# Value and ones products of the causal attention cores: five blocks a group become two

## The chip, the cores and the metric

One NeuronCore of a Trainium2 chip runs the whole kernel in one launch. The metric is the device time of a run in microseconds; what is compared is the median over several runs. Five engines work side by side, each through its own queue in order, and wait for each other by semaphores: TensorE (matrix products into eight PSUM banks), VectorE, ScalarE, GpSimd, and SyncE, which only issues DMAs. A product reads a stationary operand of up to 128 rows and 128 columns, and its output has as many partitions as the stationary operand has columns.

## The reference, cut to what matters

A decoder block on x of shape (4, 512, 512), float32:

```
x = x + causal_attention(layernorm(x), 16 heads of 32)            # "first"
x = x + cross_attention(layernorm(x), ctx, 32 heads of 16)        # "cross"
h = x + causal_attention(rms(x) * w, rotary q and k, 16 heads)    # "rotary", biases on q, k, v
x = h + experts(rms(h)) + shared_expert(rms(h))                   # top 2 of 8, and one shared
```

A causal attention is, per batch and head,

```
scores = q @ k.T / sqrt(32), masked where key > query
out    = softmax(scores) @ v
```

and a projection by a 512 x 512 matrix follows over all heads.

## The kernel before, in words

For each attention there is a projection phase (q, k, v, stored to memory as high and low parts) and a core phase, `core_phase` (line 915). The change lies in the core phase of the two causal ones, "first" and "rotary"; the code is shared with "cross".

A causal core works through 16 groups (`GROUPS`): 4 batches times 4 sets of 4 heads. A group has 16 steps, one for each pair of key tile m (0 to 3, 128 keys each) and head j (0 to 3), `step = 4 * m + j`. All engines run the same loop over groups and steps, and the order on TensorE is written out at lines 1286 to 1304. At each step it issues:

- `scores` (line 1152, products at L1162) of a tile 26 steps ahead: queries by keys, only for the maximum of each row. VectorE reduces it in `tile_max` (L1398; a second record, the accumulator read, ends it). Three PSUM banks hold these scores, so a score waits for the maximum of the tile three before it. Tiles are 128, 256, 384 and 512 columns wide.
- `scoresT` (line 1180, products at L1200, then the mask as a product with the identity at L1203): the transposed scores of this group with the row maxima subtracted through extra rows of the stacks. The keys' tile m has 512 - 128 m queries left; for m = 2 two heads and for m = 3 all four share one bank and one step (steps 8, 10, 12). ScalarE takes the exponential (L1350) into `prob_of[m]`. Three further banks rotate over these, the transposed maxima and the output projections (`share_banks`).
- at step 8, `max_transpose` (L1176) of the next group's maxima. GpSimd splits them first (`split_max`, L1597 and L1599), ScalarE copies them out (L1319) and broadcasts them by a DMA at step 9 into the next group's stack (`send_max`, L1097), which the next group's first `scoresT` waits for.
- blocks of **value products** (`values`, line 1231, L1241): four heads, each 32 output columns, so that together they fill the 128 partitions of bank 5; key tile m covers 512 - 128 m query columns, accumulated over m. Every float32 product shows as two records, so a block is 8 records.
- blocks of **ones products** (`ones_product`, line 1206, L1209): the same form with ones in place of v, the softmax's sums, into bank 6. `sums_of_first` takes key tile 0's first 128 queries; `sums` takes the other 384 columns from `total`, in which GpSimd adds the probabilities of all key tiles (`add_keys`, L1579). In the last group `sums_at_end` takes the sums straight from the probabilities, tile by tile.
- `project` (L1258): the output projection of the batch before, in thirds of four products, at steps 6, 7, 10 and 12, 14, 15 of the second and third group of a batch (the first batch has none before it).

VectorE follows a group's sums: at step 5 it flips the sums out of bank 6 (`flip_sums`, L1413), at step 6 it inverts and transposes them (`normalise`, L1420, L1423), at step 7 it scales bank 5 into `attn` (`scale`, L1433). The first value product of a group waits for that scaling of the group before, and the first ones product for the flip.

Which block stands where is set by `VALUES_LAG = 9` and `SUMS_STEP = 4` (line 987) through `values_behind` (line 1006): key tile 0 behind step 9 (with `sums_of_first`), tile 1 behind step 13, tile 2 behind step 1 of the next group, tile 3 behind step 5, and `sums` behind step 4. A step's scores and transposed scores are issued before its block.

```
VALUES_LAG, SUMS_STEP = 7 if cross else 9, 4
n, beat = divmod(g * N16 + step - VALUES_LAG, HEADS_AT_ONCE)
return divmod(n, TT) if beat == 0 and 0 <= n < GROUPS * TT else None
```

SyncE loads the stacks (`next_stack`, L213) three groups ahead, once the last transposed score of the group whose slot they take has run (step 12), and stores the projected rows (`store`, L1115); the order on its queue is fixed. ScalarE loads values (L1082), residual rows (L1090) and output weights.

Of the kernel before, what the change touches and what calls it, by code (L numbers as in the profile page):

```python
# [26 lines left out]
TT = S // P  # L27
# [887 lines left out]
def core_phase(nc, s, c, psum, a):  # L915
# [6 lines left out]
    cross, causal, dh, G = t.cross, t.causal, t.dh, t.groups  # L922
    BODY = a.body
    GROUPS = G * BODY
    N16 = TT * HEADS_AT_ONCE
    ctx = ExitStack()
    with ctx:
# [56 lines left out]
        PACKED = {2: 2, 3: 4} if causal else {}  # L984
        heads_in = lambda step: PACKED.get(step // HEADS_AT_ONCE, 1)
        leads = lambda step: step % heads_in(step) == 0
        VALUES_LAG, SUMS_STEP = 7 if cross else 9, 4
        bank_score, bank_shared = ((0, 1, 2, 3), (4, 5, 7)) if cross else ((0, 1, 2), (3, 4, 7))
        bank_o, bank_sum = (6, 6) if cross else (5, 6)
        N_SCORE = len(bank_score)  # L990
# [9 lines left out]
        def scores_before(step):  # L1000

            if cross:
                return range(step - 2, step + 2) if step % HEADS_AT_ONCE == 2 else ()
            return (step,)

        def values_behind(g, step):

            n, beat = divmod(g * N16 + step - VALUES_LAG, HEADS_AT_ONCE)
            return divmod(n, TT) if beat == 0 and 0 <= n < GROUPS * TT else None

        def probability(g, m, j):

# [4 lines left out]
        def tile_ahead(g, step):  # L1017

            n = g * N16 + step + AHEAD
            return divmod(n, N16) if n < GROUPS * N16 else None  # L1020
# [41 lines left out]
        with nc.Fori(0, B // BODY) as loop:  # L1062
            rows = lambda m, bi: m[bass.ds((loop * BODY + bi) * S, S), :].rearrange("(t p) d -> p t d", p=P)
            with nc.Block() as block:
# [86 lines left out]
                def _(pe):  # L1151
                    def scores(g, i):

                        m, j = divmod(i, HEADS_AT_ONCE)
                        n, slot = g * N16 + i, g % STACK_SLOTS
                        at, r = j // HALVES, j % HALVES * HALF_ROWS
                        bank = psum[bank_score[n % N_SCORE]]
                        if i == 0:
                            pe.wait_ge(stack_loaded[slot], 16 * (a.stacks_before + t.loads_of_stack * (g // STACK_SLOTS + 1)))
                        if n >= N_SCORE + EARLY:  # L1160
                            pe.wait_ge(s.max_done, maxima_made(n - N_SCORE) + 1)
                        last = nc.tensor.matmul(bank[:, 0 : width_q(m)], q_stack[slot][r : r + PRODUCT_ROWS, at, m * P : (m + 1) * P],  # L1162
                                                k_stack[slot][r : r + PRODUCT_ROWS, at, 0 : width_q(m)], start=True, stop=True)
                        last.then_inc(s.scores_ready, 1)
# [7 lines left out]
                    def max_transpose(g):  # L1172
                        pe.wait_ge(s.max_split, 2 * g)
                        free_bank(("max", g))
                        for m in range(TT):
                            last = nc.tensor.transpose(psum[bank_at["max", g]][0 : 2 * HEADS_AT_ONCE, m * P : (m + 1) * P],  # L1176
                                                       max_parts[:, m, :].bitcast(F32), c.ident[:])
                        last.then_inc(s.max_transposed, 1)

                    def scoresT(g, i):  # L1180

                        if not leads(i):
                            return
                        m, j0 = divmod(i, HEADS_AT_ONCE)
                        n, slot, heads = g * N16 + i, g % STACK_SLOTS, heads_in(i)
                        bank, q0 = psum[bank_at["score", n]], start_k(m)
                        tiles = bank[:, 0 : heads * (S - q0)].rearrange("p (h n) -> p h n", h=heads)
                        if i == 0:
                            if g == 0:
                                pe.wait_ge(a.carried.picks_here, 16 * (a.picks_before + HALVES * t.slots_at_hand))  # L1190
                            if g == t.slots_at_hand:
                                pe.wait_ge(s.picks_loaded, 16 * HALVES * (STACK_SLOTS - t.slots_at_hand))
                            if g:
                                pe.wait_ge(s.max_loaded, 16 * HALVES * g)
                            else:
                                pe.wait_ge(a.carried.max_here, 16 * (a.max_before + HALVES))
                        free_bank(("score", n))
                        for h in range(heads):
                            at, r = (j0 + h) // HALVES, (j0 + h) % HALVES * HALF_ROWS
                            last = nc.tensor.matmul(tiles[:, h], k_stack[slot][r : r + ALL_ROWS, at, m * P : (m + 1) * P],  # L1200
                                                    q_stack[slot][r : r + ALL_ROWS, at, q0:S], start=h == 0, stop=not causal)
                        if causal:
                            last = nc.tensor.matmul(tiles[:, :, 0:P], c.ident_r[:], c.earlier_r[:].unsqueeze(1).to_broadcast([P, heads, P]), start=False, stop=True)  # L1203
                        last.then_inc(s.scoresT_ready, heads)

                    def ones_product(columns, probabilities, **ends):

                        for j in range(HEADS_AT_ONCE):
                            last = nc.tensor.matmul(psum[bank_sum][32 * j : 32 * j + 32, columns], c.ones[:], probabilities[:, j], **ends)  # L1209
                        last.then_inc(s.sums_done, 1)  # L1210

                    def sums_of_first(g):

                        pe.wait_ge(s.exp_done, g * N16 + HEADS_AT_ONCE)
                        if g:
                            pe.wait_ge(s.flip, g)
                        ones_product(slice(0, P), prob_of[0][:, :, 0:P], start=True, stop=True)

                    def sums(g):

                        pe.wait_ge(s.added, (TT - 1) * (g + 1))
                        ones_product(slice(P, S), total[:], start=True, stop=True)
# [8 lines left out]
                    def values(g, m):  # L1231

                        q0, h0, n_load = start_k(m), (g % G if cross else 0) * HEADS_AT_ONCE, g // G if cross else g
                        if m == 0 and (g % G == 0 or causal):
                            pe.wait_ge(v_loaded[n_load % V_SLOTS], 16 * (TT if cross else 1) * (n_load // V_SLOTS + 1))
                        pe.wait_ge(s.exp_done, g * N16 + (m + 1) * HEADS_AT_ONCE)
                        if m == 0 and g:
                            pe.wait_ge(s.flip if cross else s.attn_out, g)
                        for j in range(HEADS_AT_ONCE):
                            val = v[:, n_load % V_SLOTS, m, 32 * (h0 + j) : 32 * (h0 + j + 1)]  # L1240
                            last = nc.tensor.matmul(psum[bank_o][32 * j : 32 * j + 32, q0:S], val, probability(g, m, j), start=m == 0, stop=m == TT - 1)  # L1241
                        last.then_inc(s.pv_done, 1)
# [43 lines left out]
                    for g in range(GROUPS):  # L1286
                        for step in range(N16):
                            for ahead in scores_before(step):
                                if tile_ahead(g, ahead):
                                    scores(*tile_ahead(g, ahead))  # L1290
                            scoresT(g, step)
                            if step == MAX_STEP and g + 1 < GROUPS:
                                max_transpose(g + 1)
                            if values_behind(g, step):
                                g_v, m_v = values_behind(g, step)
                                values(g_v, m_v)
                                if causal and g_v == GROUPS - 1:
                                    sums_at_end(m_v)
                                elif causal and m_v == 0:
                                    sums_of_first(g)  # L1300
                            if causal and g and step == SUMS_STEP:
                                sums(g - 1)
                            if projected_at(g, step):
                                project(*projected_at(g, step))
                    for step in range(VALUES_LAG):
                        if values_behind(GROUPS, step):
                            g_v, m_v = values_behind(GROUPS, step)
                            if causal:
                                sums_at_end(m_v)
                            values(g_v, m_v)  # L1310
# [1101 lines left out]
```

## Time and profile before

| what | value |
|---|---|
| median of 3 runs | 2159.01 us (2152.72 to 2161.05) |
| the profiled run's own time | 2174.66 us |
| its span | 2172.9 us |
| mean granted TensorE clock | 0.958 |
| TensorE busy | 2018.2 us (93%) |
| TensorE weight loads | 1340.0 us (62%) |
| VectorE, ScalarE, GpSimd busy | 1214.0, 873.1, 697.4 us |
| DMA | 297.64 MB, mean 137 GB/s |

The profile is of one execution. Times inside it count from the start of its span. The first core runs from about 190 to 425 us, the cross core to about 1000 us, the rotary core from about 1196 to 1425 us, the experts to the end. Products on TensorE are pipelined: the start of a product against the start of the one before it says what it cost, its duration does not. "[0.53 <- X]" behind a row is idle time of the engine just before it, and what ended it. The granted clock is a share of 2.4 GHz; a stretch at half of it runs at 1.2 GHz.

### The profile page before, as it was taken

To read this page: it belongs to the slowest core of one execution; us is meant where nothing else is said; L and a number is where in the kernel's file an instruction comes from. 1 tells how busy PE (TensorE), PEld (TensorE's weight loads), DVE (VectorE), ACT (ScalarE), POOL (GpSimd) and SP (SyncE) were. 2 spreads that over 40 slices of the span, in tenths; PEclk is the share of its full clock that TensorE was granted. 3 is DMA by queue.
4 is the path that set the end of the run, shared out by engine and by line. 5 is a ranking of instruction groups with operands and counts; after the bars stand their busy time and mean duration, and the time that the engine had idled before them with its cause. 6 is when DMAs were issued, how large, how long until landed. Compare 5 with 4: busy or idle time off the path is not lost. (4 is left out here: it accounts for less than half of the span.)

```text
span 2172.9 us, 31103 instructions
## 1 busy us (share of the span) xinstructions
PE 2018.2 (93%) x10519; PEld 1340.0 (62%) x10519; DVE 1214.0 (56%) x2649; ACT 873.1 (40%) x1535; POOL 697.4 (32%) x610
## 2 busy tenths in 40 slices
PE   7998999978799999997998899979999998999998
PEld 6875666666433334334776566657878787565664
DVE  6555766566799898875886666644323153222221
ACT  3424444355377676773443444434222221111111
POOL 0003665346423232322664755601000000232332
PEclk9998998989899999997998899989999999999999
DMA  5637676356754646444466767452112055233331
GB/s 199 222 138 187 159 158 140 104 185 250 255 145 118 152 105 154 100 127 128 173 222 205 166 162 160 121 213 105 54 44 78 1 218 208 45 60 60 66 61 36
DMA packets 150832, 297.64 MB, mean 137 GB/s; under 512 B 24594, under 2 KB 43156, under 8 KB 149588
## 3 DMA queue, kind: packets, MB, share of 16 engines
q1 hardware_dynamic: 112900, 242.29, 37.6%
q10 hardware_dynamic: 29040, 34.74, 6.2%
q0 software_dynamic: 8736, 18.62, 4.6%
q8 instruction: 86, 1.41, 0.3%
q14 instruction: 70, 0.57, 0.1%
HBM read 181.55 MB, written 102.50 MB: 131 GB/s over the span
## 5 line engine op out<-in xcount | busy, mean ns | idle before, releaser
L1353 ACT ACTIVATE cross_c_prob<-bank 128x512 f32<-128x512 f32 x512 | 271.1, 598 | 118.9 <-PE bank L1200 117.6
L1402 DVE TENSOR_REDUCE row_max<-bank 128x2 f32<-128x1024 f32 x248 | 290.7, 1213 | 24.6 <-PE bank L1162 23.6
L1860 PE MATMUL bank<-moe_hT,moe_w 128*128 128x512 f32 x1056 | 250.6, 393 | 7.7 <-DVE moe_w L2103 7.7
L1200 PE MATMUL bank<-stack 56*128 56x512 f32 (+4 forms) x768 | 225.7, 437 | 11.9 <-DMA stack<-first_c_max_rows 3.9
L1860 PEld LDWEIGHTS bank<-moe_hT,moe_w 128*128 128x128 f32 x1056 | 199.4, 190 | 50.1 <-issue 7.9
L1162 PE MATMUL bank<-stack 48*128 48x512 f32 (+4 forms) x720 | 184.9, 441 | 26.0 <-PEq L71 13.6
L1200 PEld LDWEIGHTS bank<-stack 56*128 56x128 f32 (+1 forms) x768 | 114.9, 197 | 142.8 <-ACT cross_c_prob L1353 68.5
L1948 PE MATMUL bank<-moe_w_e,moe_hT_e 128*128 x624 | 194.2, 465 | 6.2 <-DMA moe_w_e<-in_experts_packed 5.9
L1948 PEld LDWEIGHTS bank<-moe_w_e,moe_hT_e 128*128 128x128 f32 x624 | 116.4, 191 | 67.3 <-issue 9.6
L1162 PEld LDWEIGHTS bank<-stack 48*128 48x128 f32 (+1 forms) x720 | 92.0, 196 | 101.4 <-DVE row_max L1402 46.1
L1398 DVE CUSTOM_DVE_ANT_0 first_c_masked<-bank,later 128x128 f32<-128x128 f32 (+3 forms) x240 | 110.2, 486 | 75.9 <-PE bank L1162 73.5
L1350 ACT ACTIVATE first_c_prob<-bank 128x512 f32<-128x512 f32 (+1 forms) x176 | 95.6, 559 | 130.3 <-PE bank L1203 129.3
L1398 DVE CUSTOM_DVE_ANT_0 rotary_c_masked<-bank,later 128x128 f32<-128x128 f32 (+3 forms) x240 | 109.9, 485 | 66.5 <-PE bank L1162 64.1
L1350 ACT ACTIVATE rotary_c_prob<-bank 128x512 f32<-128x512 f32 (+1 forms) x176 | 95.4, 559 | 124.5 <-PE bank L1203 121.8
L1241 PE MATMUL bank<-cross_c_prob,cross_c_v 128*32 128x512 f32 x1024 | 141.2, 625 | 0.6 <-DVE cross_c_flipped L1413 0.6
L1816 POOL DMA_INDIRECT out_x<-moe_res,moe_token x39 | 61.9, 1586 | 231.2 <-ACT moe_res L2056 231.2
L2227 DVE TENSOR_TENSOR moe_prod<-moe_prod,bank 128x512 f32<-128x512 f32 x44 | 30.3, 688 | 180.8 <-PE bank L1860 180.8
L1871 PE MATMUL bank<-moe_w,moe_inner 128*128 128x512 f32 x528 | 128.5, 393 | 0.0
L1799 POOL TENSOR_TENSOR moe_res<-moe_res,moe_x_tile 128x512 f32<-128x512 f32 x16 | 22.6, 1413 | 312.0 <-DMA moe_x_tile<-x 312.0
L2273 DVE TENSOR_TENSOR moe_inner_e<-moe_silu_e,bank 128x352 f32<-128x352 f32 x39 | 20.3, 521 | 166.8 <-ACT moe_silu_e L2063 166.8
L1871 PEld LDWEIGHTS bank<-moe_w,moe_inner 128*128 128x128 f32 x528 | 98.7, 188 | 21.1
L1967 PE MATMUL bank<-moe_w_e,moe_innerT 128*128 (+1 forms) x234 | 107.0, 593 | 0.8 <-DVE moe_innerT L2279 0.8
(391 smaller groups left out, 3987.5 us busy)
## 6 DMA issues: line engine op xcount, KB each, us to landing
moe_w_e<-in_experts_packed SPq DMA_DIRECT2D x8, 2176.0 KB, 8.9
qk_parts<-first_p_parts SPq DMA_DIRECT2D x32, 512.0 KB, 2.6
stack<-qk_parts SPq DMA_DIRECT2D x64, 256.0 KB, 7.1
qk_parts<-cross_p_parts SPq DMA_DIRECT2D x32, 512.0 KB, 2.7
stack<-qk_parts SPq DMA_DIRECT2D x256, 64.0 KB, 2.6
qk_parts<-rotary_p_parts SPq DMA_DIRECT2D x32, 512.0 KB, 2.7
moe_raw<-in_shared_packed SPq DMA_DIRECT2D x11, 768.0 KB, 8.4
stack<-qk_parts SPq DMA_DIRECT2D x16, 512.0 KB, 6.3
```

Source lines behind the costliest of these rows:

```text
L1162: last = nc.tensor.matmul(bank[:, 0 : width_q(m)], q_stack[slot][r : r + PRODUCT_ROWS, at, m * P : (m + 1) * P], k_stack[slot][r : r + PRO ...
L1200: last = nc.tensor.matmul(tiles[:, h], k_stack[slot][r : r + ALL_ROWS, at, m * P : (m + 1) * P], q_stack[slot][r : r + ALL_ROWS, at, q0:S] ...
L1241: last = nc.tensor.matmul(psum[bank_o][32 * j : 32 * j + 32, q0:S], val, probability(g, m, j), start=m == 0, stop=m == TT - 1)
L1350: nc.scalar.activation(prob_of[m][:, j : j + heads], psum[bank_at["score", n]][:, 0 : heads * (S - q0)].rearrange("p (h n) -> p h n", h=he ...
L1353: nc.scalar.activation(probability(g, m, j), psum[bank_at["score", n]][:, 0:S], ACT.Exp).then_inc(s.exp_done, 1)
L1398: nc.vector.tensor_tensor_reduce(out=masked[:, n % 2, 0 : width_q(m)], in0=bank[:, 0 : width_q(m)], in1=c.later[:, S - width_q(m) : S], sc ...
L1402: nc.vector.tensor_reduce(row_max[:, g % 2, m, j - 1 : j + 1], c.banks[:, first : first + WIDE, :], AX_X, ALU.max).then_inc(s.max_done, 1)
L1816: pool.indirect_dma_start(a.out, bass.IndirectOffsetOnAxis(ap=token[:, t : t + 1], axis=0), y[:, t % 2, :], None, bounds_check=B * S - 1, ...
L1860: last = nc.tensor.matmul(psum[bank][:], weights(pa, f, k), hT[p % 2][:, pb, k, :], start=m == 0, stop=m == len(steps) - 1)
L1871: last = nc.tensor.matmul(psum[SD[t]][:], inner[:, n % 2, pa, t * P : (t + 1) * P], w_d(pb, f), start=f == 0 and m == 0, stop=f == KF - 1 ...
L1948: last = nc.tensor.matmul(psum[1 + 2 * (t % 2) + half][:, 0:FE], hT_e[:, t % 2, k, :], rhs, start=k == 0, stop=k == KD - 1)
L1967: last = nc.tensor.matmul(psum[6 + t % 2][:], innerT[0:kn, t % 2, n, :], rhs, start=n == 0, stop=n == len(FE_K) - 1)
```

## The change

In the causal cores the blocks behind steps 9 and 13 become one, behind step 13: value products of key tiles 0 and 1, then `sums_of_first`. The blocks behind steps 1, 4 and 5 become one, behind step 4 of the next group: value products of key tiles 2 and 3, then `sums`. `values_behind` now returns a list. In the last group the order inside a block is value products of a tile, then its sums; what is left behind the last group (key tiles 2 and 3) stands there in one piece, as before. The cross core keeps its order (lag 7).

```diff
-        VALUES_LAG, SUMS_STEP = 7 if cross else 9, 4
+        VALUES_LAG = 7
+        VALUES_AT = {13: (0, (0, 1)), 4: (1, (2, 3))}
...
         def values_behind(g, step):
 
+            if causal:
+                back, tiles = VALUES_AT.get(step, (0, ()))
+                return [(g - back, m) for m in tiles if g >= back]
             n, beat = divmod(g * N16 + step - VALUES_LAG, HEADS_AT_ONCE)
-            return divmod(n, TT) if beat == 0 and 0 <= n < GROUPS * TT else None
+            return [divmod(n, TT)] if beat == 0 and 0 <= n < GROUPS * TT else []
...
-                            if values_behind(g, step):
-                                g_v, m_v = values_behind(g, step)
+                            for g_v, m_v in values_behind(g, step):
                                 values(g_v, m_v)
                                 if causal and g_v == GROUPS - 1:
                                     sums_at_end(m_v)
-                                elif causal and m_v == 0:
-                                    sums_of_first(g)
-                            if causal and g and step == SUMS_STEP:
-                                sums(g - 1)
+                                elif causal and m_v == 1:
+                                    sums_of_first(g_v)
+                                elif causal and m_v == TT - 1:
+                                    sums(g_v)
                             if projected_at(g, step):
                                 project(*projected_at(g, step))
                     for step in range(VALUES_LAG):
-                        if values_behind(GROUPS, step):
-                            g_v, m_v = values_behind(GROUPS, step)
+                        for g_v, m_v in values_behind(GROUPS, step):
                             if causal:
                                 sums_at_end(m_v)
                             values(g_v, m_v)
```

## Rows read from the trace of the kernel before

**Rows 1.** Busy by stretch: us, PE, PEld, DVE, ACT, POOL, clock, DMA share, GB/s

```profile
300.00:400.00 100.00, 97.17 (x672) 65.81 (x671) 64.13 (x231) 44.13 (x83) 53.18 (x38) 0.92 0.55 132
...
1300.00:1400.00 100.00, 96.58 (x725) 65.62 (x726) 68.21 (x254) 46.81 (x90) 60.73 (x41) 1.00 0.66 153
```

**Rows 2.** Waits of TensorE, 195 to 420 us: total us, times, longest

```profile
PE bank L1241 <- DVE first_c_attn L1433: 3.5, 6, 0.9
```

**Rows 3.** Timeline of TensorE, first core, group without projection; start us, us, what

```profile
239.44 0.50 PE L1162 MATMUL bank<-stack 96*128 96x512 f32 x1
...
239.96 0.23 PE L1203 MATMUL bank<-earlier_r,ident_r 128*128 128x128 f32 x1
240.11 0.43 PE L1241 MATMUL bank<-first_c_prob,first_c_v 128*32 128x128 f32 x8
240.47 0.33 PE L1162 MATMUL bank<-first_k_stack,first_q_stack 96*128 96x128 f32 x1
...
240.85 0.23 PE L1203 MATMUL bank<-earlier_r,ident_r 128*128 128x128 f32 x1
240.92 0.28 PE L1162 MATMUL bank<-first_k_stack,first_q_stack 96*128 96x128 f32 x1
...
241.83 0.60 PE L1176 MATMUL bank<-ident,first_c_max_parts 128*8 128x128 f32 x4
242.18 0.31 PE L1162 MATMUL bank<-first_k_stack,first_q_stack 96*128 96x128 f32 x1
243.02 1.07 PE L1241 MATMUL bank<-first_c_prob,first_c_v 128*32 128x512 f32 x8 [0.53 <-DVE first_c_attn L1433]
...
244.23 0.39 PE L1162 MATMUL bank<-first_k_stack,first_q_stack 96*128 96x256 f32 x1
...
244.81 0.40 PE L1162 MATMUL bank<-first_k_stack,first_q_stack 96*128 96x256 f32 x2
...
245.94 0.85 PE L1241 MATMUL bank<-first_c_prob,first_c_v 128*32 128x384 f32 x8
246.72 0.79 PE L1162 MATMUL bank<-first_k_stack,first_q_stack 96*128 96x384 f32 x3
247.35 0.40 PE L1200 MATMUL bank<-stack 104*128 104x512 f32 x1
...
251.67 0.50 PE L1162 MATMUL bank<-first_k_stack,first_q_stack 96*128 96x512 f32 x1
```

**Rows 4.** Timeline of VectorE, same group: ends of three row maxima

```profile
242.16 0.08 DVE L1398 DVE_READ_ACCUMULATOR2_ANT row_max<- 128x1 f32 x1
...
242.99 0.08 DVE L1398 DVE_READ_ACCUMULATOR2_ANT row_max<- 128x1 f32 x1
...
243.20 0.08 DVE L1398 DVE_READ_ACCUMULATOR2_ANT row_max<- 128x1 f32 x1
```

**Rows 5.** Timeline of GpSimd, same group

```profile
241.23 0.22 POOL L1599 TENSOR_TENSOR first_c_max_parts<-row_max,first_c_max_parts 128x16 fp32r<-128x16 f32 x1
...
245.75 3.80 POOL L1579 TENSOR_TENSOR first_c_total<-first_c_total,first_c_prob 128x1024 f32<-128x1024 f32 x2 [0.20 <-ACT first_c_prob L1350]
```

**Rows 6.** Timeline of ScalarE, same group: issue of the maxima's broadcast

```profile
243.17 0.71 ACTq L1097 DMA_DIRECT2D stack<-first_c_max_rows  x1
```

**Rows 7.** Timeline, first core, group with projection

```profile
255.93 0.60 PE L1176 MATMUL bank<-ident,first_c_max_parts 128*8 128x128 f32 x4
...
256.18 0.60 ACT L1350 ACTIVATE first_c_prob<-bank 128x512 f32<-128x512 f32 x1 [1.00 <-PE bank L1203]
```

**Rows 8.** Timeline, last group of a batch: SyncE, ScalarE's queue and TensorE

```profile
345.81 0.34 SPq L1115 DMA_DIRECT2D x<-first_c_out_t  x1
346.20 0.59 SPq L213 DMA_DIRECT2D first_q_stack<-qk_parts  x1
...
352.84 0.73 ACTq L1097 DMA_DIRECT2D stack<-first_c_max_rows  x1
...
358.94 0.50 PE L1200 MATMUL bank<-stack 104*128 104x512 f32 x1 [1.76 <-DMA stack<-first_c_max_rows]
```

## The prediction

> **What bounds the kernel now.** The change touches only the two causal attention cores (first and rotary), so I looked there. First the busy time by stretch [rows 1]: inside either core TensorE is busy 97 of 100 us, VectorE 64 to 68, ScalarE 44 to 47, GpSimd 53 to 61. TensorE's queue sets the pace, and a nanosecond taken out of it counts unless another engine's product is then late. Second, what TensorE waits for [rows 2]: the first core loses 3.5 us, in six groups, to VectorE's scaled attention (L1433), which the first value product of a group needs. Third, the timeline of one group that carries no output projection [rows 3]; it repeats in both cores. Read the starts, not the durations, which overlap. A whole group takes 12.23 us there (sums end at 239.44, next sums end at 251.67).
>
> **What a block costs beyond its columns.** Value and ones products write 32 output columns of the array, all others 128. Both blocks of 8 records carry the same work per column: 128 columns take 0.36 us from start to the next product (240.11 to 240.47), 384 take 0.78 (245.94 to 246.72). The slope is 0.21 us per 128 columns and 0.15 us is left over at zero columns. The pair 512 plus 128 (243.02 to 244.23, 1.21 us) is the test: five slopes are 1.05, and one leftover makes 1.20. Adjacent blocks thus share one leftover, although each half has its own semaphore increment. Going in costs as well: from a mask product to a block 0.15 us, to another full-width product 0.07, so 0.08 more [rows 3]. One trip into the 32-column form and back costs 0.15 + 0.08 = 0.23 us.
>
> TensorEngine Tiling (Array Packing) in the Trainium skill, Key Properties, says that changing the tiling mode drains the engine, while a change of tile alone does not; rows 3 agree (0.23 us against none between blocks). TensorE: Matmul & The Clock Gate in the Trainium skill, Part 2, puts an isolated product's fixed cost at about 0.166 us at full clock; taken twice per trip it would be an estimate of 0.33 us, and the part of the gain that is trips would be about 40% larger. The rows decide.
>
> **Part by part.** Work is neither added nor removed: five trips a group (steps 9, 13, 1, 4, 5) become two (13, and 4 of the next group). Three trips fewer are 3 x 0.23 = 0.70 us a group. No DMA is moved; semaphores count in the same order.
>
> *Group without projection, by hand, zero at the end of the sums (239.44).* Before, the transposes of the maxima start at 2.39. The 128-column block of step 5 goes (0.36 + 0.08), which would give 1.94, but the maxima's low part on GpSimd is ready only at 241.45, that is 2.01 [rows 5]: it hangs on VectorE's last 512-column maximum, behind the flip, itself behind the sums. Transposes at 2.07, so 0.13 us of new wait. Step 9's score follows at 2.42 (0.35 as before) and no block comes behind it; the wait for L1433 is gone (0.53). But now steps 10 to 12 run into the three score banks: each score needs the maximum three tiles back, and these sit around VectorE's reciprocal, transposition and scaling. They are done at 2.80, 3.63 and 3.84 [rows 4]. Step 10 starts at 2.86 instead of about 2.54, step 11 at 3.69 (0.58 behind step 10 would be 3.44), step 12 at 3.90 instead of 3.81. The rest to the block takes 1.13 us in rows 3, so the block of step 13 starts at 3.69 + 1.13 + 0.09 = 4.91. It holds 512, 384 and 128 columns: 1.21 + 0.63 = 1.84, end 6.75. Before: 7.28 (246.72). Gain 0.53. Steps 14 to 4: the block of 256 leaves step 1, the block of 128 joins: 768 columns in one block are 6 x 0.21 + 0.15 = 1.41 against 0.57 + 0.08 + 0.78 = 1.43. Without the block at step 1 VectorE's maxima still keep up: it has no other work there, and the queue already paused for it at the same three scores before. **Gain 0.55 us a group**, of 1.23 (0.70 and 0.53) that TensorE's side offers.
>
> *Group with projection (6 of 16: second and third of a batch but the first).* No wait for L1433 there, 8 more full-width stretches, so VectorE has time. With step 9 empty, step 10's transposed score needs the bank that the exponential of step 8 frees. That runs from 0.25 to 0.85 us behind the first transpose [rows 7], free at about 0.91; TensorE is there at 0.35 plus two short scores, 0.57 to 0.69 (an estimate from 0.58 for 1,024 columns, and with starts). I take 0.25 us of wait; the ends are 0 and 0.6 (ScalarE's copy of the maxima first). **Gain 0.45.**
>
> *Where a DMA ends the wait.* In the last group of a batch the next group's first transposed score waits 1.76 us for the broadcast of the maxima, issued at 352.84, used at 358.94: 6.1 us [rows 8]; elsewhere the same transfer is in time 4.2 us behind its issue (243.17 [rows 6], used at 247.35 [rows 3]). SyncE issued the stacks late there (346.20), behind the store of the last projected tile (345.81), and they fill the queues. Nothing in this change makes them earlier: gain 0, range 0 to 0.4. TensorE just waits longer.
>
> *The new sums position.* The keys' sum on GpSimd ends at 249.55, 10.1 behind zero [rows 5]; the sums now start near 6.75 + 3.5 + 0.63 = 10.9. It is covered by 0.8 us; without that cover each group would lose what exceeds it. Flip and scaling follow the sums as before, scaling needs no later value product. ScalarE's right to overwrite probabilities 2 and 3 comes with step 4, wanted at steps 8 and 12. Cost 0.
>
> **Sum per core.** Six projecting groups x 0.45 = 2.7. Four undisturbed others (fourth of the first batch, first of each later batch) x 0.55 = 2.2. Two stalled: 0. Third group, where GpSimd splits output weights before the maxima: 0.25, one trip. Last group, three trips to two and part of the L1433 wait: 0.5. First two, largely on loads: 0.3. Together 5.95, both cores 11.9 us. The profiled run took 2174.66 us (span 2172.9); it would take 2162.8. The median of the runs shown, 2159.01, is 0.7% below it; the difference carries over: **2147 us**.
>
> **Rivals.**
> 1. *The gain comes through whole.* No new waits: 15 groups x 0.70 + 3.5 = 14 us a core, 28 in all, 2131 us. For: TensorE's 97%. Against: the banks' arithmetic above.
> 2. *VectorE and ScalarE swallow it.* The same chains, with the wait for the step-8 exponential at 0.7 instead of 0.25 and 0.5 us more at steps 10 to 12 of the other groups. What is left is about 3 us: 2156. For: VectorE's flip, transposition and scaling stand in a row there. Against: at the steps of the new blocks it idles. TensorEngine Tiling in the Trainium skill, PSUM Bottleneck, warns that packed products move the bound to emptying PSUM; rows 1 show VectorE far from that on average, rows 4 close to it for two microseconds of each group.
> 3. *Slower, by the maxima's DMA.* Step 12 now comes earlier against the maxima's broadcast, and step 12 releases SyncE's next stacks (1.6 us earlier on the group's clock, 4.9 instead of 6.3 to 6.5). If they hold up the broadcast as in rows 8 (6.1 us), the four undisturbed groups a core start their next at 3.4 + 6.1 = 9.5 (the issue was at 3.73 and moves with the transposes) instead of 7.9: 8 x 1.6 = 12.8 us lost against 7.5 us kept elsewhere, 2164. It decides from 4.0 us of latency on (next group's start then at 6.75 + 0.63 = 7.4). The granted clock adds to it: the stretch with such a wait ran at 0.92 of full speed, the same stretch of the other core at 1.00 [rows 1], which is 16 us at 1.2 instead of 2.4 GHz, or 8 us, some 4 per long wait; with half of eight, 2180. Against: the earlier stacks also have longer to land before the next broadcast.
>
> **How the numbers follow.** Forecast (gain of 6 to 18 us) 0.50, rival 1 0.13, rival 2 0.27, rival 3 0.10. A measurement of this kernel tells 0.5%, 10.8 us, from no change. Of the forecast's half some 0.33 lies beyond it; with rival 1 that is 0.47 for faster. Slower takes 0.08 of rival 3, the rest, 0.45, is within. The forecast's own range is 2141 to 2153; the range to hold 8 in 10 runs from rival 1's 2131 to just beyond rival 2, 2161, with the clock's few microseconds in it.
>
> **What would show it.** In the changed profile: blocks of 24 records at steps 13 and 4; no wait on L1433; period of a plain group 11.7 us (full gain 11.0, swallowed 12.1); first transpose 2.07 us behind the sums, waiting for L1599; new waits of 0.1 to 0.3 us on L1398 at steps 10 to 12 and on L1350 at step 10 of projecting groups; the broadcast stall above 2 us in the last group of a batch. I am wrong if the plain period does not fall, if sums wait for L1579, or if groups other than those now show the DMA of the maxima.

## The result, and the profile after

| | before | after |
|---|---|---|
| median of 20 runs | 2162.7 us | 2149.5 us |
| ratio, 95% interval | | 0.9935 (0.9922 to 0.9947) |
| profiled run, span | 2172.9 us | 2150.7 us |
| first core phase, in the profile | 257.8 us | 248.8 us |
| rotary core phase | 252.6 us | 247.3 us |

A core phase is counted from the first to the last instruction of a computing engine in it.

The medians are 13.2 us apart, the ratio says 0.65%, or 14.1 us; 11.9 us were forecast. (The forecast's 2147 us is 2.5 below the measured median all the same: it starts from the median of three runs before, 2159.0, where twenty gave 2162.7.) The two profiled runs are 22.2 us apart, but only 14.3 of that lies in the two causal cores. The rest is in phases that the change does not touch (the cross core 424.1 to 420.8 us, the first projection 164.8 to 162.5, the third 163.8 to 162.2): the profiled run of before lies 12 us above the median of its kernel.

Not all of the 14.3 us is the change's either. In the profile of before the ninth and the thirteenth group of the first core, each behind a wait of 1.8 to 1.9 us for the maxima's broadcast, ran at a mean granted clock of 0.77 and 0.61, parts of them at 1.2 GHz instead of 2.4. They took 15.14 and 17.64 us; the same two groups of the rotary core, at full clock, took 12.12 and 12.15. In the changed kernel's profile two of these four fell, to 0.77 and 0.87 (14.68 and 13.16 us against 11.64). That is some 8.5 us of clock before and 4.6 after.

The page of the changed kernel: the engines' busy time (share of the span, instructions), and the granted clock in forty slices. The instruction counts are those of before.

```profile
PE 1999.7 (93%) x10519; PEld 1349.4 (63%) x10519; DVE 1208.1 (56%) x2649; ACT 869.7 (40%) x1535; POOL 696.1 (32%) x610
...
PEclk9997999989899999998998999989999999999999
```

Next, what TensorE waited for in the first core (us in total, times, longest).

```profile
PE bank L1166 <- DMA first_k_stack<-qk_parts: 3.4, 1, 3.4
PE bank L1204 <- DMA stack<-first_c_max_rows: 3.0, 2, 1.9
PE bank L1180 <- POOL first_c_max_parts L1601: 2.1, 1, 2.1
PE bank L1204 <- ACT first_c_prob L1352: 0.7, 2, 0.4
```

The wait for the scaled attention is gone [rows 2]. GpSimd's split of the maxima (L1180) costs 2.1 us in one place, the third group, where GpSimd also splits the output weights. The wait of a transposed score for ScalarE's exponential is new (0.7 us in the two that are listed). The broadcast of the maxima still stalls TensorE at two places.

The timeline of TensorE from the end of the sums in the fourth group to the end of the sums in the fifth, both without projection, against [rows 3] (there one group later; such a group took 12.24 us before):

```profile
228.20 0.50 PE L1166 MATMUL bank<-stack 96*128 96x512 f32 x1
228.54 0.34 PE L1204 MATMUL bank<-first_q_stack,first_k_stack 104*128 104x384 f32 x1
...
229.70 0.33 PE L1166 MATMUL bank<-stack 96*128 96x128 f32 x1
...
230.28 0.60 PE L1180 MATMUL bank<-ident,first_c_max_parts 128*8 128x128 f32 x4
230.63 0.77 PE L1166 MATMUL bank<-stack 96*128 96x128 f32 x2
...
231.86 0.59 PE L1166 MATMUL bank<-stack 96*128 96x256 f32 x2
...
233.18 1.71 PE L1245 MATMUL bank<-first_c_prob,first_c_v 128*32 128x512 f32 x16
234.71 0.40 PE L1213 MATMUL bank<-first_c_prob,ones 128*32 128x128 f32 x8
235.04 0.79 PE L1166 MATMUL bank<-stack 96*128 96x384 f32 x3
235.67 0.40 PE L1204 MATMUL bank<-stack 104*128 104x512 f32 x1
...
237.34 0.45 PE L1166 MATMUL bank<-stack 96*128 96x512 f32 x1
237.63 0.39 PE L1204 MATMUL bank<-stack 104*128 104x512 f32 x1
...
238.54 0.86 PE L1245 MATMUL bank<-first_c_prob,first_c_v 128*32 128x256 f32 x16
...
239.97 0.50 PE L1166 MATMUL bank<-stack 96*128 96x512 f32 x1
```

and the ends of the maxima on VectorE that gate steps 10 to 12, against [rows 4]:

```profile
230.88 0.08 DVE L1400 DVE_READ_ACCUMULATOR2_ANT row_max<- 128x1 f32 x1
...
231.72 0.08 DVE L1400 DVE_READ_ACCUMULATOR2_ANT row_max<- 128x1 f32 x1
...
231.93 0.08 DVE L1400 DVE_READ_ACCUMULATOR2_ANT row_max<- 128x1 f32 x1
```

Zero is 228.20, the end of the sums. Step 8's score starts at 1.50, the transposes at 2.08, where the last score bank and the split let them (2.39 before). The row at 230.63 merges two scores; the second starts at 231.02, or 2.82, and the row's 0.77 us for two 128- and 256-column products shows the wait in it. Step 11 starts at 3.66. Their banks are freed by the maxima ending at 230.96, 231.80 and 232.01, that is 2.76, 3.60 and 3.81. Then one block of 16 + 8 records from 4.98 to 6.84, and at 238.54 the other, 1.43 us to 239.97. The group ends at 11.77.

Three waits can be read from this: 0.24 us between the scores of steps 9 and 10 (230.63 to 231.02 is 0.39; the changed kernel's 128-column score behind the transposes takes 0.14 where nothing is waited for), 0.26 ahead of step 11's score (the mask product of step 10 takes 0.38 until it instead of 0.12) and 0.19 ahead of step 12's.

In a group with projection (the sixth; columns as above, TensorE and ScalarE), against [rows 7]:

```profile
255.45 0.60 PE L1180 MATMUL bank<-ident,first_c_max_parts 128*8 128x128 f32 x4
...
255.69 0.60 ACT L1352 ACTIVATE first_c_prob<-bank 128x512 f32<-128x512 f32 x1 [1.00 <-PE bank L1207]
...
255.80 0.48 PE L1166 MATMUL bank<-first_k_stack,first_q_stack 96*128 96x128 f32 x2
...
256.34 0.51 PE L1204 MATMUL bank<-stack 104*128 104x256 f32 x2
```

Step 8's exponential starts 0.24 us behind the first transpose, as before. The row at 255.80 merges the scores of steps 9 and 10; the second starts at 255.94. A 256-column score takes 0.12 us until the next product where nothing is waited for (two take 0.24, 244.81 to 245.05 in the trace of before), so the transposed score of step 10 could have started at 256.06. It starts at 256.34, 0.89 behind the first transpose: it waits 0.28 us, until the exponential ends at 256.29. Its two products then take 0.34 us instead of 0.24 until the mask product, so the wait costs 0.38.

The same place before, where a block stands behind step 9, TensorE's rows:

```profile
256.28 0.31 PE L1162 MATMUL bank<-first_k_stack,first_q_stack 96*128 96x128 f32 x1
256.52 1.07 PE L1241 MATMUL bank<-first_c_prob,first_c_v 128*32 128x512 f32 x8
...
257.73 0.39 PE L1162 MATMUL bank<-first_k_stack,first_q_stack 96*128 96x256 f32 x1
257.95 0.40 PE L1200 MATMUL bank<-stack 104*128 104x256 f32 x2
```

The trip costs 0.09 us on the way in (0.24 from the score to the block, 0.14 from the same score to the next one in the changed kernel), 0.14 in the block (1.21 here; moved behind step 13 the same products add 1.07 us to the block there, 1.86 against 0.78), and 0.10 on the score behind it (0.22 instead of 0.12): 0.33 us.

The stalled group, SyncE's queue, ScalarE's queue and TensorE, against [rows 8]:

```profile
281.78 0.34 SPq L1119 DMA_DIRECT2D x<-first_c_out_t  x1
...
282.16 0.59 SPq L213 DMA_DIRECT2D first_q_stack<-qk_parts  x1
...
288.47 0.71 ACTq L1101 DMA_DIRECT2D stack<-first_c_max_rows  x1
...
293.85 0.50 PE L1204 MATMUL bank<-stack 104*128 104x512 f32 x1 [1.17 <-DMA stack<-first_c_max_rows]
```

Again the stacks go out (282.16) behind the store of the last projected tile (281.78), the broadcast takes 5.4 us, and TensorE idles 1.17 us in front of the next group.

### The profile page after: what moved, and what is told of

Read it like the earlier page. It is cut to its first block and busy times, and to the rows that moved or that the text cites. A ratio compares the mean times of both kernels' runs of the same rounds, so it can differ in the third digit from the quotient of the medians.

```text
span 2150.7 us, 31103 instructions
## 1 busy us (share of the span) xinstructions
PE 1999.7 (93%) x10519; PEld 1349.4 (63%) x10519; DVE 1208.1 (56%) x2649; ACT 869.7 (40%) x1535; POOL 696.1 (32%) x610
## 5 line engine op out<-in xcount | busy, mean ns | idle before, releaser
L1204 PE MATMUL bank<-stack 56*128 56x512 f32 (+4 forms) x768 | 223.2, 432 | 11.7 <-DMA stack<-rotary_c_max_rows 4.2
```

## The experiments

**Once more, as the reference for the next three**, on their chip.

> The changed kernel itself, on the chip of the three runs beside it. Both theories: 13 to 14 us below the kernel before (ratio 0.9935); groups without projection 11.76 us, with projection 16.5 to 16.7.

2150.4 us, ratio 0.9926 (0.9905 to 0.9947). Periods of the first core: fifth group 11.77, sixth 16.76, eleventh 16.53 us. As expected.

**Each half alone.** The groups' periods are what these runs are for; the whole time moves by little more than its interval. A period is the distance between the first 512-column transposed scores of two groups.

```diff
-        VALUES_AT = {13: (0, (0, 1)), 4: (1, (2, 3))}
+        VALUES_AT = {13: (0, (0, 1)), 1: (1, (2,)), 5: (1, (3,))}
...
-                                elif causal and m_v == TT - 1:
-                                    sums(g_v)
+                            if causal and g and step == 4:
+                                sums(g - 1)
```

> Only the front is joined: key tiles 0 and 1 and the first ones product behind step 13; tile 2 stays behind step 1, the sums behind step 4, tile 3 behind step 5. Theory A (the step by step walk: in a group without projection the VectorE maxima of steps 10 to 12 fix where the step-13 block can start, in one with projection the step-8 exponential does): a group without projection takes 11.7 us, as in the full change, one with projection about 16.95; 6 to 8 us faster than before in all (ratio 0.997). Rival B (every trip saved is worth its 0.23 us wherever it is, and the removed wait 0.5): both kinds of group gain one trip, 11.5 and 16.8, and in all 15 us (0.993), more than the full change's half.

Measured: 2163.9 us, ratio 0.9988 (0.9966 to 1.001). Starts of the fifth, sixth and seventh group, first core:

```profile
237.00 0.39 PE L1204 MATMUL bank<-stack 104*128 104x512 f32 x1
...
248.82 0.40 PE L1204 MATMUL bank<-stack 104*128 104x512 f32 x1
...
266.10 0.39 PE L1204 MATMUL bank<-first_q_stack,first_k_stack 104*128 104x512 f32 x1
```

11.82 us without projection and 17.28 with. Joining the front is worth 0.42 us in the one (before: 12.24) and nothing in the other (before: 17.24). For groups with projection both theories were wrong (16.95 and 16.8 expected): the trip's 0.33 us goes to the wait for the exponential, whose cost is 0.38. The whole time, expected at 0.997, moved by 0.12%, within its interval. In this profile, too, the thirteenth group of the first core ran at a mean clock of 0.55, behind a wait of 2.9 us for the broadcast, and took 18.76 us.

```diff
-        VALUES_AT = {13: (0, (0, 1)), 4: (1, (2, 3))}
+        VALUES_AT = {9: (0, (0,)), 13: (0, (1,)), 4: (1, (2, 3))}
...
-                                elif causal and m_v == 1:
+                                elif causal and m_v == 0:
                                     sums_of_first(g_v)
```

> Only the back is joined: tiles 2 and 3 and the sums behind step 4; tile 0 stays behind step 9, tile 1 behind step 13. Theory A: in a group without projection the two trips saved are lost again, since step 9's block still waits for the scaled attention (3.58 us behind the sums, as before): 12.2 us, the wait for it grows from 0.53 to about 0.85 with 0.13 of new wait for GpSimd's split; with projection both trips count, 16.55. In all 5 to 6 us faster (0.9975). Rival B: two trips in every group, 11.8 and 16.55, 14 us (0.9935).

Measured: 2155.3 us, ratio 0.9955 (0.994 to 0.997). The same three starts, and the wait for the scaled attention in the first core:

```profile
237.76 0.40 PE L1204 MATMUL bank<-stack 104*128 104x512 f32 x1
...
249.93 0.40 PE L1204 MATMUL bank<-stack 104*128 104x512 f32 x1
...
266.61 0.40 PE L1204 MATMUL bank<-first_q_stack,first_k_stack 104*128 104x512 f32 x1
```

```profile
PE bank L1245 <- DVE first_c_attn L1435: 7.5, 9, 1.1
```

12.17 us without projection, 16.68 with: two trips saved are worth 0.07 in the one and 0.56 in the other. Where projections leave VectorE time, both trips count; where they do not, what is saved at steps 1 to 5 comes back as a longer wait for the scaled attention, 7.5 us against the 3.5 of [rows 2]. So trips are not worth the same everywhere, and rival B of these runs, a gain of 0.4 us for the two trips in a group without projection too, falls.

| period, us | before | front only | back only | both (the change) |
|---|---|---|---|---|
| fifth group, no projection | 12.24 | 11.82 | 12.17 | 11.76 |
| sixth, projection | 17.24 | 17.28 | 16.68 | 16.71 |
| eleventh, projection | 17.01 | 17.05 | 16.44 | 16.53 |

**One trip put back.** The first ones product stands alone again, behind step 14.

```diff
-                                elif causal and m_v == 1:
-                                    sums_of_first(g_v)
...
+                            if causal and step == 14 and g < GROUPS - 1:
+                                sums_of_first(g)
                             if projected_at(g, step):
```

> The changed kernel with one trip more: the first ones product stands alone behind step 14. Same products. Theory A: 0.23 us more in each group with projection (16.75), 0.05 to 0.1 in one without, where TensorE waited anyway for a score bank at step 1 (11.85); in all about 4 us slower than the changed kernel. Rival B: 0.23 us in all groups, 7 us slower. Rival C (a trip has no price, the gain is the removed wait and other order alone): no difference.

Measured: 2155.1 us, ratio 0.9956 (0.9941 to 0.997), 4.6 us above the changed kernel. Starts of the eleventh and twelfth group in it, and, in the second fence, of the sixth, eleventh and twelfth in the changed kernel:

```profile
323.03 0.40 PE L1204 MATMUL bank<-first_q_stack,first_k_stack 104*128 104x512 f32 x1
...
339.86 0.40 PE L1204 MATMUL bank<-first_q_stack,first_k_stack 104*128 104x512 f32 x1
```

```profile
247.43 0.40 PE L1204 MATMUL bank<-stack 104*128 104x512 f32 x1
...
322.20 0.40 PE L1204 MATMUL bank<-first_q_stack,first_k_stack 104*128 104x512 f32 x1
...
338.73 0.39 PE L1204 MATMUL bank<-first_q_stack,first_k_stack 104*128 104x512 f32 x1
```

The eleventh group takes 16.83 us instead of 16.53: with the same products, a trip costs 0.30 us. The fifth group took 11.88 (0.12 more), the tenth 16.82 (0.11 more): there 0.22 us of the trip falls into a wait for a score bank at step 1 that was there anyway (the mask product of step 0 takes 0.06 until the next score instead of 0.23). Rival C falls, and so does rival B, the same price in every group.

**VectorE out of the way.** In the changed kernel the scaled attention is needed four steps later than before, but VectorE still makes it as early as it can. The three numbers are the steps of VectorE's flip, of its reciprocal and transposition, and of its scaling; what ScalarE does behind the scaling moves along, from step 10 to 13. The kernel before ran beside this run and the two that follow, the changed kernel did not, so they are compared by their ratios.

```diff
-        FLIP_STEP, NORM_STEP, BACK_STEP = (4, 6, 8) if cross else (5, 6, 7)
+        FLIP_STEP, NORM_STEP, BACK_STEP = (4, 6, 8) if cross else (5, 8, 10)
```

> The changed kernel with VectorE's reciprocal and transposition at step 8 instead of 6, the scaling at step 10 instead of 7, and what ScalarE does behind it at 13 instead of 10; the attention of the group before is not needed until step 13 now. Theory A (in groups without projection the row maxima of steps 10 to 12 come late because those three operations stand ahead of them): the two waits for score banks of 0.27 us each go, block at 4.3 instead of 5.0 us behind the sums, period 11.1 to 11.3 instead of 11.76; groups with projection as in the changed kernel (16.5 to 16.7). Four undisturbed groups a core, 3 to 5 us in all below the changed kernel. Rival (TensorE is bound by its own products there, waits only move): no difference, 11.7.

Measured: 2152.9 us, ratio 0.9963 (0.9946 to 0.998). Starts of the fourth, fifth and ninth group:

```profile
221.81 0.39 PE L1204 MATMUL bank<-first_q_stack,first_k_stack 104*128 104x512 f32 x1
...
233.03 0.40 PE L1204 MATMUL bank<-stack 104*128 104x512 f32 x1
...
291.50 0.65 PE L1204 MATMUL bank<-stack 104*128 104x512 f32 x1 [2.15 <-DMA stack<-first_c_max_rows]
```

The mechanism is as expected: the fourth group takes 11.22 us, and the waits ahead of the scores of steps 10 and 11 are gone (0.24 and 0.26 us); the 0.19 us ahead of step 12's stay. The time is not: 3 to 5 us below the changed kernel were expected, and this one is no faster. The sixth group now waits for the broadcast of the maxima too (0.3 us), and the ninth and thirteenth of both cores wait 2.0 to 2.3 us for it, where the changed kernel's waited 1.0 to 1.9. Behind these waits all four ran at a mean granted clock of 0.76 to 0.87 and took 12.7 to 14.2 us. What VectorE gave, the DMA and the clock took.

**SyncE's order.** Without the edit to VectorE's steps: the second store of a group goes behind the next stacks.

```diff
                         if g + 3 < GROUPS:
                             next_stack(sp, g + 3)
+                        for m in late:
+                            store(sp, m)
+                        late = []
...
-                        for m in early:
+                        if causal and stores_now:
+                            late = [(g // G - 1) * TT + early[-1]]
+                        for m in early[:-1] if causal else early:
                             store(sp, (g // G - 1) * TT + m)
```

> The changed kernel with one order turned on SyncE's queue in the causal cores: of the two projected rows' stores of a group the second goes behind the next group's stack loads, not ahead of them. Theory A (the stall of 1.0 to 2.3 us at the start of the first group of a batch comes from stacks issued 5 us late behind that store): the stacks go out near step 12, the broadcast of the maxima lands in 3.4 us instead of 5.1 to 6.5, the stalled groups fall from 12.7 to 14.0 us to 11.8, 4 to 8 us in all below the changed kernel, and more where a stretch at half the clock goes too. Rival D (DMA bandwidth is the limit): the same stall whoever goes first, no difference.

Measured: 2139.6 us, ratio 0.9893 (0.9873 to 0.9914). SyncE's queue, and the starts of the eighth and ninth group:

```profile
274.69 0.59 SPq L213 DMA_DIRECT2D first_q_stack<-qk_parts  x1
...
277.28 1.64 SPq L213 DMA_DIRECT2D first_k_stack<-qk_parts  x1
280.55 0.34 SPq L1119 DMA_DIRECT2D x<-first_c_out_t  x1
```

```profile
279.75 0.39 PE L1210 MATMUL bank<-first_q_stack,first_k_stack 104*128 104x512 f32 x1
...
291.28 0.39 PE L1210 MATMUL bank<-stack 104*128 104x512 f32 x1
```

The stacks leave at 274.69, five microseconds before the eighth group starts, and the store at 280.55 follows them. The eighth group takes 11.53 us instead of 12.87, without a wait; so do the other three of its kind. This kernel beats both others, the changed one by 0.3 to 0.4 percentage points, 7 to 9 us, where 4 to 8 were expected and more if a stretch at half the clock went too. The profiles say where: from the start of the fourth group to that of the last the two cores together are 10.1 us shorter than in the changed kernel's profile. The four stalled groups give 6.1 of it. The rest is clock: none of the ninth and thirteenth groups falls below full clock here, and none did in the other three profiles with this order. Rival D (bandwidth, the same stall whoever goes first) falls for this stall.

> Both edits, VectorE's late steps and the stacks first. Theory A: the two add up, all groups without projection from the fourth on 11.1 to 11.3 us, 8 to 13 us below the changed kernel, 1.0% to 1.2% below the kernel before. If the broadcast's 3.4 us is now the next bound (needed about 3.4 to 3.5 us behind its issue), 11.3 to 11.5 and a small wait for it in each of them.

Measured: 2141.5 us, ratio 0.9894 (0.9875 to 0.9912). Both edits together, and no diff beyond the two above; 8 to 13 us below the changed kernel were expected. It is no better than the stacks alone. The twelfth group took 11.00 us, but two of them in a row are too much: from the issue of the broadcast in the ninth group to the start of the tenth,

```profile
299.00 0.71 ACTq L1101 DMA_DIRECT2D stack<-first_c_max_rows  x1
...
303.81 0.49 PE L1210 MATMUL bank<-stack 104*128 104x512 f32 x1 [1.13 <-DMA stack<-first_c_max_rows]
```

4.8 us and an idle engine. In the rotary core the tenth group starts 1.95 us late in the same way, at a broadcast of 5.6 us, and runs at a mean clock of 0.91 (18.18 us). Of the two sizes expected, neither held: the broadcast is late not by a little everywhere, but by up to 2 us in the second of two short groups.

**The kernel before with the stacks first**, the same SyncE edit on five blocks.

> The kernel before, five blocks a group, with only SyncE's order turned as in the stacks-first run. It tells what the joined blocks are worth where no stall hides them. Theory A: the stalled groups fall from 12.8 to 14.0 us to 12.0, 6 to 10 us in all below the kernel before (0.996); the joined blocks on top of it are then worth 14 to 16 us (the stacks-first run was 0.9893), a little more than the 13 to 14 without it, since the four formerly stalled groups gain their 0.5 us as well. Rival (the stalls were a product of the joined blocks): no difference to the kernel before.

Measured: 2155.0 us, ratio 0.9965 (0.9948 to 0.9983). Starts of the eighth and ninth group:

```profile
281.91 0.40 PE L1206 MATMUL bank<-first_q_stack,first_k_stack 104*128 104x512 f32 x1
...
293.91 0.40 PE L1206 MATMUL bank<-stack 104*128 104x512 f32 x1
```

12.00 us instead of 14.03, so the stalls were no product of the joined blocks. Between 0.9965 and 0.9893 lie 0.72%, or 15.5 us, give or take 6 by the two intervals: the change is worth as much here as with the stalls (14.1 us), and a difference between the two is not shown. The profiles are finer, since neither waits for the broadcast nor falls below full clock in this stretch: from the start of the fourth group to that of the last, the core phases take 174.4 and 174.3 us here, 168.9 and 168.7 with joined blocks, 5.5 and 5.6 us less.

> The stacks-first run, with the front joined only in groups without projection; in those with projection tile 0 stays behind step 9 and tile 1 with the first ones product behind step 13. Theory A: a group with projection takes 16.44 to 16.68 us as in the back-only run, against 16.53 to 16.76, since the trip more (0.23) fills the wait of 0.18 for the step-8 exponential and for a score bank at step 1; in all at most 1 us apart from the stacks-first run. Rival B (a trip is 0.23 us everywhere): 3 us slower than it.

```diff
+        VALUES_APART = {9: (0, (0,)), 13: (0, (1,)), 4: (1, (2, 3))}
...
-                back, tiles = VALUES_AT.get(step, (0, ()))
+                back, tiles = (VALUES_APART if g >= G and g % G in (1, 2) else VALUES_AT).get(step, (0, ()))
```

Measured: 2141.1 us, ratio 0.9914 (0.9884 to 0.9944), the same as the stacks first within the interval, which cannot tell the 3 us of rival B from none. The periods can: the eleventh group took 16.43 us against 16.53, the seventh of the first core 16.43 against 16.83, the fifteenth 15.03 against 15.29. So a trip more costs nothing in front of that exponential, as expected, and a little is even to be had: from the fourth group to the last the two cores are 1.9 us shorter, too little to show in the whole.

## Why the prediction was right, point by point

**TensorE's queue sets the pace, and a trip has a price: right, the price too low.** The prediction read 0.23 us from the leftover of a block (0.15) and the way in (0.08). Back-only gives 0.57 for two trips (17.01 to 16.44), the trip put back 0.30. The part that was missed is the first product behind the block. It can be seen in the changed kernel's timeline: the first 512-column score behind a block, at 228.20, is followed by the next product 0.34 us later, the one behind a mask product, at 237.34, after 0.29. A trip in the back thus costs 0.28. At the front no mask product stands between the scores, the score behind the block loses 0.10, and the trip costs 0.33. Three trips are 0.90 us a group, not 0.70. The drain that the Trainium skill names (TensorEngine Tiling (Array Packing), Key Properties) agrees with it that each trip has a price; the 0.33 us estimated from two isolated products' fixed costs is the front's price and above the other two (0.28, 0.30), and that the price is made up that way is not shown.

**A group without projection: 11.77 us against 11.7 forecast,** and each term of the walk stands in the rows above. Transposes 2.08 (2.07 forecast), step 10 at 2.82 (2.86), step 11 at 3.66 (3.69), block at 4.98 (4.91), its end 6.84 (6.75). The gain is 0.47, not 0.55. TensorE's side offered more than the 1.23 us of the prediction, about 1.5: three trips at 0.90, and 0.60 for the wait for the attention. The new waits took more as well, about 1.0: 0.17 at steps 7 and 8 for a score bank and GpSimd's split, 0.05 at steps 1 to 3, and the rest around steps 9 to 12. That VectorE's reciprocal, transposition and scaling are behind the largest of them was confirmed from the other side: moving these made the group 11.22 us.

**A group with projection: gain 0.48 to 0.53 against 0.45.** The cause was right, and the size is in part luck: two errors nearly cancel. The trips were worth 0.90, not 0.70. The wait for the exponential was 0.28 us, near the 0.25 taken, but it cost 0.38, since the products behind a wait start slowly, and scores at steps 1 to 3 lost 0.04 to score banks: 0.90 - 0.38 - 0.04 = 0.48. The front's trip alone is thus a small loss here, as front-only shows. The ends 0 and 0.6 of the wait held it, the upper one closely: in the seventh group of the first core it was 0.59 us, and that group gained only 0.17. There the exponential starts 0.56 us behind the first transpose instead of 0.24, with ScalarE's copy of the maxima still behind it; why was not looked into.

**The stalled groups: gain 0 forecast.** 14.03, 13.93, 12.81 and 12.99 us before, 12.87, 13.56, 13.11 and 12.73 after; the repeated run had 12.66, 14.01, 13.23 and 12.79. All of them ran at full clock; they vary with the DMAs by more than the change could give. That TensorE would just wait longer, above 2 us, did not come true: it waited 1.0 to 1.9 us, and 0.7 to 1.9 before. The cause was argued from two rows on SyncE's queue, and the reordering showed it. What the prediction had among its rivals only, the clock behind such a wait, weighs nearly as much as the stall: the group that follows lost 1.5 to 5.5 us where the clock fell.

**The last group: 0.5 forecast, 1.0 to 1.1 measured,** and this is the term that was mis-sized. From its first 512-column score to the end of the core phase it took 23.9 us before and 22.8 after; front-only has 22.8, back-only 24.2, so it is the front. Its wait for the scaled attention was 0.86 us, not 0.5, and with one trip that is the whole. "Part of the L1433 wait" should have been read from that group.

**The third group: 0.25 forecast, not found.** It took 12.96 and 15.41 us before, 15.85 and 16.63 after, but 12.37 and 13.10 in the repeated run of the same kernel. TensorE waits there for GpSimd (2.1 to 2.3 us, 1.3 to 2.0 before) and the granted clock then falls in some executions and not in others (a mean of 0.79 in the groups of 15.85 and 16.63 us, 1.00 in those of 12.96 and 12.37). What of it the change adds is open; it was not tried alone.

**The sum.** Per core, six groups of about 0.48 (the last of them 0.28, where the exponential is waited for 0.3 us longer; in the first core also one of 0.17), four of about 0.5 and the last group's 1.1 are 5.6 to 5.8 us, both cores 11.4. The other 2 to 3 us may be in the first three groups or in the clock, and lie within the interval (11.5 to 16.9 us); which was not shown. That the total of 11.9 us came so close is partly luck: the trips and the last group were taken too low, the waits too low as well, and 0.55 us a core were put down to the first three groups, whose times vary by more than that.

**The rivals.** The whole gain (2131 us) failed on the waits of steps 10 to 12. Being swallowed (2156) needed waits of 0.7 us for the exponential; it was 0.28, and came near that only in the seventh group of the first core. The broadcast's delay by stacks released earlier did not come about in this kernel: it used to be ready 3.2 us behind its issue, and now takes 3.4. But it was the right thing to fear: with VectorE's steps moved as well, the groups got short enough for it, and the gain was gone. The fall of the clock that rival 3 priced at some 4 us behind a long wait is real (1.5 to 5.5 us), but it follows the waits at the end of a batch, before the change as after it, and made no new ones here.

## What to carry to other kernels

On a queue that is 97% busy, the price of a reordering can be walked: for each moved block, ask which bank, buffer or reader the instruction behind it needs, and who frees it. Price the block with the product behind it, too: that one was missed here. Saved time counts only until the next such resource; in the same kernel the same saving was worth all (0.57 of 0.57 us) in groups where another stage left slack, and a tenth of it (0.07) in the others. And look at what already stalls before tuning further: one store moved behind a load was worth half of this change to two thirds (7 to 9 us), and about two fifths of it was clock that TensorE no longer lost behind the stalls. A short wait can cost more than its own length.

## What had not been expected

Joining blocks freed a deadline (the scaled attention was needed at step 13 instead of 9) that paid in full only once VectorE's order used it, and then the group of 11.0 to 11.2 us met the DMAs: two short groups in a row make a broadcast of 64 KB take 4.8 to 5.6 us instead of 3.4. The DMA engines were nearly full while they did: during those two broadcasts the DMA share (their packets' times added up; it can pass 1) was 0.87 and 1.01 and 194 and 196 GB/s were moved, in the changed kernel's stalled ones 1.10 to 1.12 and 192 to 227, and in those of its fourth and fifth group, which took 3.4 to 3.6 us, 0.47 and 0.68 at 107 and 154 GB/s. (One of 3.4 us had 0.86 and 189 GB/s, so a full queue does not always delay it.) Whether the amount of traffic or the order of the queues decides was not tried.
